# One core's Mamba-2 mixer kernel: the off-chunk product ahead of the token transposes in every slot

## The reference

```python
hBC = silu(conv(hBC))                                   # depthwise, 4 taps
X = hs * dt                                             # per head and token
A_cs = cumsum(A * dt)                                   # inside a chunk of 128 tokens
M = (Cc @ Bc.T) * exp(segsum(A_dt))                     # inside a chunk
Y_diag = M @ X
states = (Bc * exp(A_cs[-1] - A_cs)).T @ X              # one per chunk
prev_states = running sum of states with decay          # from chunk to chunk
Y_off = (Cc @ prev_states) * exp(A_cs)                  # chunks 1, 2, 3
y = Y_diag + Y_off + D * hs
out = x + rms_norm_by_group(y * silu(gate)) @ out_proj.T + ffn_branch
```

## Time and profile before

| | us |
|---|---|
| median of 3 runs | 1635.52 (1633.87 to 1637.02) |
| the profiled execution, whole | 1635.75 |
| its span in the trace | 1634.0 |
| PE busy | 1611.7 (99%) |
| DVE busy | 1383.7 (85%) |
| ACT busy | 1263.2 (77%) |
| POOL busy | 1150.4 (70%) |
| DMA engines, mean of 16 | 40.8% |

### The profile page before, as it was taken

The page is one execution under the profiler, slowest core; times in us unless marked ns, Lnnn a source line. Parts: engine busy times, 40 slices in busy tenths (PEclk is TensorE's granted clock), DMA queues, the critical chain, the costliest instruction groups (busy, mean ns, idle before and its releaser), DMA issues.

```text
span 1634.0 us, 28969 instructions
## 1 busy us (share of the span) xinstructions
PE 1611.7 (99%) x9662; PEld 1352.2 (83%) x9662; DVE 1383.7 (85%) x2342; ACT 1263.2 (77%) x2489; POOL 1150.4 (70%) x1472
## 2 busy tenths in 40 slices
PE   8999999999999999999999999999999999999998
PEld 6778888888888888888778788888888888888887
DVE  6988888888888888898889888888888888888887
ACT  3578887888888887888746788888788888888785
POOL 5348687777777776868763577768777777777684
PEclk9999999999999999999999999999999999999999
DMA  5244434444444444344314444443444444444431
GB/s 172 84 141 127 148 121 140 134 128 148 126 135 145 128 136 137 123 149 125 122 40 145 121 148 131 130 148 124 138 135 127 147 129 132 145 129 136 136 124 62
DMA packets 82308, 212.18 MB, mean 130 GB/s; under 512 B 11120, under 2 KB 27504, under 8 KB 81904
## 3 DMA queue, kind: packets, MB, share of 16 engines
q1 hardware_dynamic: 82160, 210.33, 40.8%
HBM read 207.14 MB, written 3.15 MB: 129 GB/s over the span
## 4 chain that ended last, share of the span: by engine, by line
PE 91%; DVE 5%; POOL 1%; issue 1%; ACT 1%; DMA 0%; POOLq 0%; DVEq 0%
PE bg L634 22%; PE bo L780 21%; PE bh L634 12%; PE bt L634 11%; PE by L833 8%; PE bg L853 5%; PE bh L825 3%; PE bt L825 3%; PE bh L841 2%; PE bt L841 2%; DVE cv L877 1%; PE bg L759 1%; PE bo L634 1%; PE bo L691 1%; DVE sq L877 1%
## 5 line engine op out<-in xcount | busy, mean ns | idle before, releaser
L596 POOL TENSOR_TENSOR xl<-xg,xh 128x256 fp32r<-128x256 f32 x254 | 290.5, 1165 | 332.9 <-ACT xh L460 332.1
L529 POOL TENSOR_TENSOR wl<-raw,wh 128x256 fp32r<-128x256 f32 x584 | 425.6, 759 | 106.0 <-ACT wh L319 106.0
L347 ACT ACTIVATE mt<-cs_row,cs_tok 128x128 f32<-128x128 f32 x1024 | 324.8, 391 | 0.0
L610 POOL TENSOR_TENSOR wol<-raw_o,woh 128x256 fp32r<-128x256 f32 x256 | 181.9, 732 | 31.0 <-ACT woh L449 31.0
L780 PE MATMUL bo<-woh,xh 128*128 128x512 f32 x512 | 200.9, 392 | 1.7 <-POOL xl L596 1.7
L1107 DVE TENSOR_TENSOR mt<-mt,gt 128x1024 f32<-128x1024 f32 x128 | 201.8, 1577 | 0.3 <-ACT mt L495 0.3
L780 PE MATMUL bo<-woh,xl 128*128 128x512 f32 x512 | 200.3, 391 | 0.0
L780 PE MATMUL bo<-wol,xh 128*128 128x512 f32 x512 | 200.0, 391 | 0.0
L603 POOL TENSOR_TENSOR sqa<-sqa,sq 128x256 f32<-128x256 f32 x222 | 159.1, 736 | 0.9 <-ACT sq L477 0.9
L319 ACT ACTIVATE wh<-raw 128x1024 fp32r<-128x1024 f32 (+1 forms) x146 | 152.1, 1041 | 0.7 <-DMA raw<-in_w_dtag 0.7
L460 ACT ACTIVATE xh<-xg 128x512 fp32r<-128x512 f32 x128 | 81.0, 633 | 89.1 <-DVE xg L1087 89.1
(11 more groups left out here) (192 smaller groups left out, 3576.9 us busy)
## 6 DMA issues: line engine op xcount, KB each, us to landing
raw<-in_w_step SPq DMA_DIRECT2D x128, 512.0 KB, 3.5
cs_row<-cs_rows SPq DMA_DIRECT2D x128, 512.0 KB, 5.4
raw_o<-in_w_out SPq DMA_DIRECT2D x128, 256.0 KB, 4.1
ec_row<-ec_rows SPq DMA_DIRECT2D x256, 96.0 KB, 4.7
raw<-in_w_bc SPq DMA_DIRECT2D x16, 512.0 KB, 3.5
acc<-in_x SPq DMA_DIRECT2D x4, 512.0 KB, 5.7
cs_row<-in_w_ffn SPq DMA_DIRECT2D x2, 1024.0 KB, 6.2
out_dram<-acc SPq DMA_DIRECT2D x1, 1024.0 KB, 6.5
```

What stands on the lines that cost most here:

```text
L347: e = act.activation(mt[:, m % 2, h, chunk(j)], cs_row[:, m % 2, h, chunk(j)], ACT.Relu, bias=cs_tok[:, j, 2 * m + h:2 * m + h + 1], scale ...
L529: e = pool.tensor_tensor(wl[:, n % 2, cols], raw[:, n % 2, cols], wh[:, n % 2, cols].bitcast(F32), ALU.subtract)
L596: e = pool.tensor_tensor(xl[:, u, cols], xg[:, u, cols], xh[:, u, cols].bitcast(F32), ALU.subtract)
L610: e = pool.tensor_tensor(wol[:, 1 - u, cols], raw_o[:, 1 - u, cols], woh[:, 1 - u, cols].bitcast(F32), ALU.subtract)
```

## The change

The block with the four transposes (L841) moves behind the block with the off-chunk product (L853), in every slot. The waits stay with their blocks. Nothing else changes.

```diff
                     if m == STEPS and b + 1 < NB:
                         project_dt(b + 1)
-                    if has(m):
-                        pe.wait_ge(v_h2, did(un))
-                        for j in range(NJ):
-                            mm = pe.transpose(mine[:, chunk(j)], h2[:, u, chunk(j)], ident[:, :])
-                        mm.then_inc(t_t, 1)
                     if has(m - 1):
                         pe.wait_ge(v_sg, did(min(n, b * STEPS + STEPS - 1)))
                         pe.wait_ge(v_off, did(n - 2))
...
                             mm = pe.matmul(bg[:, chunk(c)], S[:, c, :], ct[:, g, chunk(c + 1)], start=True, stop=True)
                         mm.then_inc(t_off, 1)
+                    if has(m):
+                        pe.wait_ge(v_h2, did(un))
+                        for j in range(NJ):
+                            mm = pe.transpose(mine[:, chunk(j)], h2[:, u, chunk(j)], ident[:, :])
+                        mm.then_inc(t_t, 1)
```

## The result

| | before | after |
|---|---|---|
| median | 1635.52 us (9 runs, 1633.87 to 1638.47) | 1640.66 us (9 runs, 1640.48 to 1642.09) |
| ratio | | 1.0033, 95% interval 1.0024 to 1.0042 |
| span of the profiled execution | 1634.0 us | 1638.9 us |

The forecast was 1639.8 us. The page of after has the same shape as before: PE is busy 99% of the span and carries the chain that ended last.

What follows compares the result with a forecast made beforehand. PE's own instruction stream was taken to set the time. Stream +6.6, gate -3.7, slot 1 +0.9 and end +0.5 summed to +4.3 us on the 1635.52 us median: 1639.8 us, range 1635.0 to 1644.0.

Steps and rivals of the forecast that it cites:

- Hole and cold start: Behind L833: the 0.17 us hole stays; a cold product load replaces a cold transpose, 46 ns a slot, joints returning 3.
- second rival: Behind L833: the product's load is covered, so the 46 ns vanish; 1634.4 us, not slower; chance 0.18.
- the third: Rival: the hole behind L833 disappears too, or earlier xg lifts an unseen wait; faster by over 0.2%; chance 0.04.
- Projection behind transposes: The projection following transposes instead of the product takes 0.01 us more a slot, ends 0 and 0.02.
- Gate: Out projection's first load, held by the end of POOL's xl, is no longer gated because yo starts earlier; -3.7 us.
- Third part and its state: The off-chunk product's third part just fits behind its last state, by 0.01 to 0.02 us; taken as 0.
- first rival: The product's third part misses its state, or xl stays the gate; 1643.5 us, slower still; chance 0.14.
- Drain slots: Late states would cost 4.5 us in 14 drain slots, but earlier ACT and DVE work should cancel it; taken as 0.
- Slot 1: In slot 1 of each batch entry the transposes follow the late third part, delaying the projection 0.44 us; +0.9 us.
- End: In slot 63 of the last entry the later transposes delay DVE's xd to about 1616.9; +0.5 us.

Runs made afterwards that it cites:

- e3: Kernel after with one of the four transposes put ahead of the off-chunk product, three behind it; 1637.14 us, ratio 1.001 to before.
- e8: Kernel after with the inner product (L833) made of 128-column instead of 64-column matmuls, values of y not the reference's; 1710.75 us, one run.
- e9: Kernel before with the inner product made of 128-column instead of 64-column matmuls, values of y not the reference's; 1713.2 us, one run.
- e5: Kernel after with the four transposes put between the second and third part of the off-chunk product; 1643.21 us, ratio 1.0042 to before.
- e1: Kernel before with the out projection's wait for xl moved to its third matmul, the first that reads xl; 1630.47 us, ratio 0.9967 to before.
- e6: Kernel after with three transposes put ahead of the off-chunk product and one behind it; 1636.67 us, ratio 0.9998 to before.
- e4: Kernel after with DVE's yo additionally waiting for the transposes, taking away its head start; 1649.42 us, ratio 1.0084 to before.
- e2: Kernel after with the out projection waiting for xl only ahead of its third matmul; 1639.31 us, ratio 1.0023 to before.
- e7: Kernel after with transposes first again in slot 1 of both batch entries and slot 63 of the last; 1639.25 us, ratio 1.0018 to before.

## Why the prediction was right, point by point

- **Hole and cold start (+46 ns, less 3).** Right. The pair of records lasts as at the earlier trace rows, and the border grew from 1.082 to 1.128 us, 45 ns in the mean of the slots against my 43. The second rival falls with this and with e3, the third with the hole of 0.17 us that is still there. e8 and e9 tie the uncovered load to the 64-column block in front. I was wrong that this is the only border where no load leads: the border from L825 to L833 is another.
- **Projection behind transposes (+10, ends 0 and 20).** 16 ns: from its first to its last record 5.326 us in before and 5.342 in after. The number is inside the ends, but by luck, since the reason doesn't hold: e5 and e9 have a product directly ahead and are as slow. In all traces the first two records of a projection start 314 to 321 ns apart, and the next ones mostly 228 to 236 before they settle at 227: five distances in before and e1, eight in after, e3, e6 and e8 (one of them 224), nine in e5 and e9. What decides how many stays open.
- **Gate (-3.7 us).** Right. "Out" fell from 2.751 to 2.722, the step into it from 0.230 to 0.227 us, and e1 takes 5.0 us off the order of before by its trace, 4.1 of them in slots 2 to 63. My path to it has a wrong step without effect: `t_off` comes 0.39 us earlier, not 0.44 (the last product record starts 0.660 us behind the border's first, not 1.052), and `yo` starts 0.31 us behind that record in both kernels. So `yo` and the end of `xl` move by 0.39 us, not by the 0.33 at which I had DVE stop them.
- **Third part and its state (0).** Right, and as narrow as feared: the load starts about 65 ns behind the end of the last state in after, where one that waits starts 52 to 54 behind it. The first rival didn't happen.
- **Drain slots (0).** Right: the states are ready 0.37 us behind the first load, I said 0.39. e4 put the price of a failed cancellation at 5.2 us, I said 4.5.
- **Slot 1 (+0.9).** 0.79. From the states to the projection the two slots 1 grew by 0.43 and 0.44 us, as costed (0.44); the projection and the out projection behind it are 0.03 and 0.06 us shorter than in before.
- **End (+0.5).** 0.47. The timeline of after shows the wait that replaced DVE's readiness, against the earlier trace rows:

```profile
1618.33 0.94 PE L848 MATMUL bg<-ct,S 128*128 128x128 f32 x6
...
1619.10 0.60 PE L853 MATMUL bt<-ident,h 128*128 128x128 f32 x4
1619.74 0.56 DVE L1094 TENSOR_TENSOR xd<-bt,dd_tok 128x384 f32<-128x384 f32 x1 [0.37 <-PE bt L853]
```

The sum of the four terms was +4.3 us; the ledger has +4.85, the medians +5.1. What my sum lacks against the ledger: 124 x (45 - 43 + 16 - 10) ns = 1.0 us for the stream. Against it stand 0.1 us too much for slot 1 and a gate that gave back more than my 3.7 us: 4.1 in e1, about 3.9 as what is left of the ledger.

## What to carry to other kernels

On an engine that never waits, ask of a reordering which block will stand behind a change of the stationary operand's width, as between 64 and 128 columns here: it starts cold, and it should be the one that loses least by it (a transpose 0.056 us, the product 0.102). Look for gates that are no waits: a load that starts the same 0.05 us behind another engine's end in nearly every slot is held, even where no idle time is booked. What that costs must be measured: in before most held loads cost time, in e4 most cost none. And put a wait in front of the instruction that reads the data; here moving it by two matmuls, in e1, was worth more than either order.

## What the runs showed of the hardware

**A short stretch at a halved clock, at places that differ from one execution to the next.** The rows give the granted clock (the number ahead of DMA's share) in two stretches of each kernel; the first two are after, the last two before:

```profile
14.00:20.00 6.00, 6.00 (x28) 4.31 (x27) 1.56 (x2) 3.37 (x5) 6.00 (x9) 1.00 0.98 297
1626.50:1630.50 4.00, 4.00 (x13) 3.08 (x12) 1.40 (x2) 1.15 (x2) 2.68 (x4) 0.57 0.00 0
```

```profile
14.00:20.00 6.00, 6.00 (x21) 4.16 (x20) 0.12 (x1) 2.88 (x4) 6.00 (x9) 0.72 0.91 271
1621.60:1625.60 4.00, 3.22 (x16) 2.54 (x16) 2.92 (x5) 1.24 (x3) 4.00 (x6) 1.00 0.01 2
```

In before, PE was granted 1.2 instead of 2.4 GHz in part of the first stretch, behind a wait of 1.83 us for DVE that ended at 13.4; after has the same wait there and kept 2.4 GHz. It fell to 1.2 GHz in the tail instead, at 1626.7, behind waits of PE of 1.34, 0.66 and 0.78 us that ended at 1621.0, 1624.3 and 1626.0; in before the same three are 0.92, 0.66 and 0.78 us, and PE kept 2.4 GHz. Each time the stretch grows by 1.5 to 1.6 us. e1 had neither, e2, e7 and e8 the one at the start, e3 one near 811 us at the batch border (0.76 of full speed over 7 us), e6 one there and one in the tail, e4 one at the start and one at the batch border, e5 one at the start and one in the tail, e9 one at the start and one at 851 us. Executions of one kernel differ accordingly: after's 9 runs stand at 1640.5 to 1640.7 (six) and 1642.0 to 1642.1 (three). This is why e6 measured above its slots, and probably why e3 did; and it is why differences of 1 us between medians say little here while slots in the trace agree to 1 ns. Whether the change makes the tail's drop likelier, by its longer wait, is open.

**Gates make slots uneven.** Ungated, 94 slots agree within 2 ns (after, e1, e3, e6); gated, they spread from 11.140 to 11.207 us (before), since a load that is 0.05 us late costs anything from 0 to 0.06 us; in e4, with loads 0.09 us late, 53 of the 94 last 11.200 us as in after.
